# One transfer for the identity and the small tables, and a new order of the work around the first projection

## The reference, cut to what matters

```python
def _layernorm(x): return (x - mean(x)) / sqrt(var(x) + eps)

def attn(x, ln_w, ln_b, w_q, w_kv, w_o, theta):     # 16 heads of 16
    h = layernorm(x) * ln_w + ln_b
    q, k, v = h @ w_q, *split(h @ w_kv)
    q, k = rope(q, theta), rope(k, theta)            # angles: position * theta / 220 * fixed frequencies
    qk = einsum('bhkd,bhqd->bhkq', q, k) * 0.25
    t = 1 + qk + 0.5 * qk * qk                       # in place of exp
    attn = t / sum(t, -1)
    return einsum('bhkq,bhqd->bhkd', attn, v) @ w_o

def ffn(x, weight, bias):                            # both operands are rounded to a 6-bit grid,
    return dequant(x) @ dequant(weight).T + bias     # in blocks of 32 with a scale each

x = x + _layernorm(attn(_layernorm(x), ...))
x = x + _layernorm(ffn(_layernorm(x), weight, bias))
```

## Time and profile before

| | us |
|---|---|
| median of three runs | 634.89 |
| profiled execution | 634.73 |
| its span, first to last instruction | 632.9 |
| PE busy | 607.2 |
| DVE busy | 579.3 |
| ACT busy | 534.0 |
| POOL busy | 393.8 |

### The profile page before, as it was taken

The page is one execution under the profiler, slowest core; times in us unless marked ns, Lnnn a source line. Parts: engine busy times, 40 slices in busy tenths (PEclk is TensorE's granted clock), DMA queues, the critical chain, the costliest instruction groups (busy, mean ns, idle before and its releaser), DMA issues.

```text
span 632.9 us, 22530 instructions
## 1 busy us (share of the span) xinstructions
PE 607.2 (96%) x7588; PEld 470.3 (74%) x7588; DVE 579.3 (92%) x1425; ACT 534.0 (84%) x1505; POOL 393.8 (62%) x597
## 2 busy tenths in 40 slices
PE   8799999999999999999999999999999999999984
PEld 8677667777777787777777777777778777778763
DVE  5999999999999999999999999999999999987796
ACT  4357769898898989989899889899898888899983
POOL 2575366676666567766766777675765767653343
PEclk9999999999999999999999999999999999999996
DMA  7101131222232232223232231323233222230201
GB/s 251 35 3 39 24 76 23 66 77 74 60 95 63 76 91 64 76 49 93 73 105 62 79 83 42 108 55 97 62 83 84 68 49 52 69 85 20 68 27 51
DMA packets 55951, 43.64 MB, mean 69 GB/s; under 512 B 7200, under 2 KB 55712, under 8 KB 55840
## 3 DMA queue, kind: packets, MB, share of 16 engines
q1 hardware_dynamic: 55024, 41.42, 24.6%
q10 hardware_dynamic: 816, 0.79, 0.4%
HBM read 18.65 MB, written 8.39 MB: 43 GB/s over the span
## 4 chain that ended last, share of the span: by engine, by line
PE 87%; ACT 5%; issue 4%; DVE 3%; POOL 1%; POOLq 0%; ACTq 0%; DVEq 0%
PE ps_f L859 12%; PE ps_mt L1032 12%; PE ps_o L930 5%; PE ps_o L924 5%; PE ps_qk L783 5%; PE ps_qk L784 5%; PE ps_qk L786 5%; PE ps_w L783 4%; PE ps_tr L883 4%; PE ps_f L924 4%; PE ps_w L786 4%; PE ps_w L784 4%; PE ps_tr L783 3%; PE ps_tr L873 3%; PE ps_tr L786 2%
## 5 line engine op out<-in xcount | busy, mean ns | idle before, releaser
L1192 ACT ACTIVATE feat<-ps_f 128x512 f32<-128x512 f32 x256 | 147.5, 600 | 13.0 <-PE ps_f L859 12.4
L678 DVE TENSOR_TENSOR kf<-kf 128x672 f32<-128x672 f32 (+1 forms) x128 | 130.4, 1023 | 1.0
L859 PE MATMUL ps_f<-qT,selr 128*128 128x512 f32 x320 | 120.4, 426 | 2.0 <-ACT feat L1192 1.2
L1032 PE MATMUL ps_mt<-kf,vp 128*32 128x153 f32 x2048 | 79.6, 296 | 1.5 <-DVE kf L678 0.5
L1787 POOL TENSOR_TENSOR rs_f<-var_f,mhalf 128x1 f32<-128x1 f32 x64 | 47.9, 749 | 47.5 <-ACT squares_f L1326 46.5
L1787 POOL TENSOR_TENSOR rs_y<-var_y,mhalf 128x1 f32<-128x1 f32 x64 | 47.3, 740 | 41.9 <-ACT squares_y L1304 41.4
L1032 PEld LDWEIGHTS ps_mt<-kf,vp 128*32 128x32 f32 x2048 | 60.3, 109 | 16.7 <-issue 14.5
L1776 POOL TENSOR_TENSOR kf<-kf 128x128 f32<-128x128 f32 x64 | 36.6, 571 | 47.2 <-DVE kf L1543 47.2
L859 PEld LDWEIGHTS ps_f<-qT,selr 128*128 128x128 f32 x320 | 55.2, 188 | 13.3 <-ACT feat L1192 5.4
L1783 POOL TENSOR_TENSOR attT_l<-att,attT_h 128x256 fp32r<-128x256 f32 x56 | 45.0, 805 | 31.1 <-ACT attT_h L1233 31.0
L678 POOL TENSOR_TENSOR kf<-kf 128x224 f32<-128x224 f32 x64 | 58.2, 909 | 3.9 <-DVE kf L1548 3.8
(11 more groups left out here) (205 smaller groups left out, 1900.3 us busy)
## 6 DMA issues: line engine op xcount, KB each, us to landing
xc<-L_attn_x SPq DMA_DIRECT2D x16, 512.0 KB, 4.0
result<-fin SPq DMA_DIRECT2D x64, 128.0 KB, 1.9
xa<-L_attn_x SPq DMA_DIRECT2D x15, 512.0 KB, 4.0
heads_out<-osb SPq DMA_DIRECT2D x224, 32.0 KB, 2.0
shares<-sums SPq DMA_DIRECT2D x112, 64.0 KB
sums<-osb SPq DMA_DIRECT2D x224, 2.0 KB
wkqv<-L_attn_w_kv ACTq DMA_DIRECT2D x2, 256.0 KB, 4.6
xa<-L_attn_x SPq DMA_DIRECT2D x1, 384.0 KB, 6.1
```

The source lines that it names most:

```text
L678: return eng.tensor_tensor(dims(row, F_MAIN, [[FW, heads], [HD, NR - 1], [1, HD]]), dims(row, F_LIN, [[FW, heads], [0, NR - 1], [1, HD]]), ...
L859: pe.matmul(ps_f[i % 2][:, :], selr[:, i], queries, start=True, stop=True).then_inc(sel_done, 1)
L1032: mm = pe.matmul(ps_mt[qd // 2][VW * h:VW * (h + 1), (qd % 2) * NF:(qd % 2 + 1) * NF], vp[:, s2, qd * HQ + h], kf[:, s2, qd * HQ + h, 0:NF ...
L1192: act.activation(feat[:, p2, i], ps_f[i % 2][:, :], ACT.Square).then_inc(squared, 1)
```

## The change

Three things change. The identity and the small tables come in one transfer of 197 floats a partition with one semaphore, `cols_in`, and all who waited for `ident_in` wait for `cols_in`. The tile of ones is set by the first memset, with a semaphore `one_set` of its own, and PE begins on that; the others count to 15. The tables `ORDER` and `IDLE` are new for all five engines, over all 64 tiles. The diff without these tables:

```diff
+def sandwich(nc, x, w_q, w_kv, w_o, weight, bias, columns, selection, out):
...
             sp.dma_start(xa[:, 0, 0:1], x_seq[0][:, 0:1]).then_inc(x0_in, 16)
-            sp.dma_start(small[:, P:NSMALL], columns).then_inc(cols_in, 16)
-            sp.dma_start(ident, identity).then_inc(ident_in, 16)
+            sp.dma_start(small[:], columns).then_inc(cols_in, 16)
...
         def _(pe):
-            pe.wait_ge(setup_pool, 16)
+            pe.wait_ge(one_set, 1)
...
             def fold_kq():
 
+                pe.wait_ge(setup_pool, 15)
                 pe.wait_ge(wkq_in, 2 * 16)
...
             def turn_z(t):
                 if t.n == 1:
-                    pe.wait_ge(ident_in, 16)
                     pe.wait_ge(cols_in, 16)
...
-            act.wait_ge(setup_pool, 16)
+            act.wait_ge(setup_pool, 15)
             act.activation(warm[:], mhalf[:], ACT.Sin)
 
             def cast_identity():
-                act.wait_ge(ident_in, 16)
+                act.wait_ge(cols_in, 16)
...
             def turn_weights():
 
-                act.wait_ge(ident_in, 16)
+                act.wait_ge(cols_in, 16)
...
         def _(pool):
+            pool.memset(one[:], 1.0).then_inc(one_set, 1)
             pool.memset(mhalf[:], -0.5).then_inc(setup_pool, 1)
...
-            pool.memset(one[:], 1.0).then_inc(setup_pool, 1)
...
-            pool.wait_ge(setup_pool, 16)
+            pool.wait_ge(setup_pool, 15)
...
                 pool.tensor_scalar(lnwn[:], lnw, -((1.0 + EPS) ** -0.5), None, ALU.mult).then_inc(ln_scaled, 1)
-                pool.wait_ge(ident_in, 16)
...
-    arrays["identity"] = identity
     arrays["columns"] = np.ascontiguousarray(np.concatenate(
-        [columns, np.broadcast_to(theta, (P, 1)), ln_w.reshape(CH, P).T, ln_b.reshape(CH, P).T], axis=1), np.float32)
+        [identity, columns, np.broadcast_to(theta, (P, 1)), ln_w.reshape(CH, P).T, ln_b.reshape(CH, P).T], axis=1), np.float32)
...
-IDLE = {"fill": (1, 1, 1, 1, 1, 1, 4, 7, 10, 14, 15, 19, 23, 45,), "drain": ()}
+IDLE = {"fill": (2, 4, 6, 6, 6, 7, 7, 7, 8, 9, 16, 23, 40,), "drain": ()}
```

More of the change, by code:

```diff
@@ L98 @@
[L98 to L102 removed]
+        "attend": ((45, 59, 65, 79, 86, 104, 112, 130, 137, 149, 168, 187, 200, 214, 227, 244, 257, 272, 286, 300, 316,
+            330, 344, 359, 374, 388, 402, 416,), (26, 40, 54, 69,), (766, 780, 794, 808, 830, 835, 855, 866, 876, 891,
+            909, 919, 926,)),
@@ new lines @@
+        "high_kq": ((3,), (), ()),
+        "high_q": ((11, 18, 25, 33, 43, 55, 63, 69, 84, 94, 106, 117, 131, 149, 171, 187, 203, 216, 234, 253, 270, 291,
+            307, 323, 341, 362, 377, 394, 412, 432, 448, 465, 484,), (-86, -63, -49, -32,), (765, 784, 802, 818, 835,
+            853, 872, 889, 906, 926, 945, 961, 978, 998, 1014, 1039,)),
+        "high_v": ((6,), (), ()),
+        "sines": ((5,), (), ()),
+        "split_ffn_weight": ((127,), (), ()),
+        "split_wo": ((13,), (), ()),
[17 rows of a table added]
@@ L414, in dims @@
     return bass.AP(ap.tensor, ap.offset + offset, [list(ap.ap[0])] + [list(d) for d in free])
-def sandwich(nc, x, w_q, w_kv, w_o, weight, bias, identity, columns, selection, out):
+def sandwich(nc, x, w_q, w_kv, w_o, weight, bias, columns, selection, out):
     NS = x.shape[0]
```

404 lines of the change are left out of this document (197 added, 207 removed), and 88 rows, old and new, of the table ORDER.

## The result

The changed kernel took 635.88 us (median of 20 runs, 633.30 to 638.31), the kernel before, run beside it, 634.19 us (median of 20, 632.41 to 635.85). The ratio is 1.0022, its 95% interval 1.0013 to 1.0032. The forecast was 632.9 against 634.89, a ratio of 0.9969, so it is wrong in sign. The profiled execution took 636.04 us, its span 634.2 against 632.9.

The account below looks back on a forecast made before the run. The prediction took PE to bound the kernel from 100 to 550 us, with DVE the bound in the first 40. An earlier start would keep 2.0 us: 634.89 - 2.0 = 632.9 us, 8-in-10 range 630.7 to 635.9.

Parts of the forecast that it names:

- PE's first 14 us: Kernel start on PE: first product at about 1.0 us instead of 2.46, fold ending at 11.1 instead of 14.56.
- The merged transfer: Columns and identity in one load at the start: lands between 4.15 and 5.6 us, taken as 4.9.
- my lower bound: Start of PE's `fold_kq`: earliest 7.4 us, in a range of 7.4 to 7.9, taken as 7.6.
- DVE: DVE's first steps: angles end at 11.0 us, `low_kq` follows without `weight_scales` between, DVE ends about 1.4 us ahead.
- The wait of `normalise_x.1` for POOL: DVE, tile 1: idle for 1.0 us until POOL's tables are done, against 0.3 before.
- The lead: At the fourth `sum_features`: PE 2.4 us ahead, DVE 1.5; of this PE keeps 2.0 us.
- my own sign: Check on the start: if the fourth `sum_features` is not earlier than 41.54 us (forecast 40.4), the start's forecast is wrong.
- From there PE's work is the same in both: Behind the fourth `sum_features`: PE's work is unchanged, with one `fill` fewer, already counted.
- On SP nothing changes in the first 26 steps: SP queue at the start: its order is unchanged there, within edits costed at nothing.
- Rival (c): Slower: the new periodic order puts `low_h` one DVE step later, doubling PE's idle time; 636.9 us, chance 0.12.
- Rival (d), the clock: Slower: TensorE's full speed comes late, so the early fold runs at the slow pace; 636.2 us, chance 0.04.
- The sum: Whole kernel: 634.89 us less the 2.0 that PE keeps gives 632.9 us.

Follow-up runs that it names:

- e2: The changed kernel with all of SP's order put back to that of the kernel before, other engines as changed: 634.55 us, ratio 1.0003 to the kernel before.
- e5: The changed kernel with its new order only up to about tile 6; behind that, and on SP throughout, the order of before: 633.47 us, ratio 0.9969.
- e17: The changed kernel, unchanged, profiled and timed a second time: 637.08 us, ratio 1.0027 to the kernel before.

## Why the prediction was wrong, step by step

- **PE's first 14 us: right.** First product at 0.98 (forecast 1.0), `turn_z.0` at 6.11 (6.2), the fold from 7.12 (7.6, bounds 7.4 to 7.9, so 0.3 before the lower one) to 10.9 (11.1). The pace rose at 6.0, so the turn and the `fill` both ran at the later pace and were through at 6.94; my lower bound had the turn at the earlier one. The last 0.19 us were a wait for ACT's `wa`, written from 6.49 to 6.88, 0.1 later than in the kernel before. `project_kq.0` at 13.13 (13.4).
- **The merged transfer: right.** The first to use it starts at 4.68 (4.9, bounds 4.2 to 5.6), 3.5 us behind its issue at 1.18. Beside the 2.9 of the columns and the 3.9 of the identity the row length that the Trainium skill names (DMA: Bandwidth & Descriptors, Specifications: at least 512 B for line rate) doesn't show: the columns' rows are 276 B and landed soonest, the identity's are 512 B and landed latest, the merged ones are 788. Their sizes differ as well (34.5, 64 and 98.5 KB), so these rows neither show that rule nor refute it.
- **DVE: right within 0.6 us.** Angles from 5.63 to 11.46 (5.05 to 11.0), `low_kq.1` at 11.97 to 12.65 (11.8 to 12.45), `stats_x.1` 12.90 (12.75), `rope_cos.0` 15.81 (16.2). The 0.6 us are x of tile 0: it landed at 3.65 where it had landed at 3.07. The wait of `normalise_x.1` for POOL was 0.36, not 1.0: the tables were not as late.
- **The lead: right in size, but not made where I counted it.** Forecast: PE 2.4 us ahead, 2.0 kept. The first `sum_features` came 0.64 us earlier (0.5), `attend.3` 2.44. The fourth `sum_features` did not come earlier (41.66 against 41.54; forecast 40.4). By then PE had done three `select` and one `project_v` more, just as counted, which is 1.3 us of work, so it was 1.2 ahead there and not 2.4. By my own sign the count of the start was wrong at that row. The rest came behind it, where I had counted nothing: from 41.6 to 100 us PE idles 0.7 us less than before (1.1 against 1.8). That the sum agrees is in part luck, and where x of tile 0 lands at 3.02, close to the 3.07 of the rows that I counted from, the lead at tile 5 is 3.0 (e2).
- **"From there PE's work is the same in both": this is the step that failed.** The work is the same, its order is not, and I costed the order of 60 tiles at nothing. The forecast would have held for e5, the kernel to which that sentence applies: 0.9969, the lead kept to 0.2 us over 57 tiles. That the ratio is the very same is luck, since e5 starts from a larger lead and pays 1.4 us at its seam. In the changed kernel the order of the middle gives back 2.5 to 3.0 us in the same places in each trace and 0.1 to 2.4 more at one place. "On SP nothing changes in the first 26 steps" is true and beside the point: the later ones were priced at nothing too.
- **Rival (c) had the outcome and its test, not the mechanism.** It said slower by the new periodic order, with PE's idle time doubled: 3.95 became 7.85 us, 6.8 in the second trace. The price it worked out (636.9) is above the measured time; it left out the end, which in this trace is 1.5 us shorter from tile 60 on. But the wait it named, `low_h` one step late, is 0.3 us once, as before. The waits that grew are DVE's for POOL's `rs_y`, PE's for `fb` and those for which the profile names nobody ("issue"), and DVE's for the sums.
- **Rival (d), the clock: no part in it.** The fold's records ran at the later pace from the first (1.10, 1.05, 1.03 and 1.05 us for its four groups, against 1.03, 1.05, 1.03 and 1.05 in the kernel before). The row of the idle products shows the pace rise at 6.0 us here, 5.0 after they began; over the 17 traces of kernels with `one` set first it rose at 3.9 to 7.1. That the moment varies from run to run is what the Trainium skill states (TensorE: Matmul & The Clock Gate, Part 1), and here rows show it.
- **The sum.** -2.44 (lead at tile 3) + 5.28 (to tile 36) - 1.52 (from there to the end) = +1.32 us, the difference of the two spans.

What stays open: which pairs of steps in the new order make the 2.5 to 3.0 us that repeat. The waits say where they surface (POOL's `rs_y` before `add_attention`, DVE's `add_bias` before `project_out`), but the runs that moved these steps took the waits away without taking the loss away. Between 205 and 375 PE's idle time also explains only 3.6 of the 5.15 us; the rest is in records that PE counts as busy. It is not waiting, but mostly what stands behind what. From the start of each `select` to the start of PE's next record (93 of them, 207 to 373 us) 25.3 us pass in the kernel before and 30.8 in the changed one, of which 2.6 are idle; behind the turns of `z` it is 4.6 and 3.0. A `sum_features` follows a `select` 15 times where it did 8 times, at 0.40 us each, where a `select` behind a `select` takes 0.26 to 0.28. e17 has the same sums to 0.2 us.

## What to carry to other kernels

A list that orders the work of several engines is one object: its start can be exchanged at a price at the seam (1.4 us twice here, 5 once), its middle can't be judged by one engine or one step. When a change brings a new start and a new order behind it, price them apart, and run the new start with the old rest first; here that kernel was the gain (0.9969), and the rest was the loss. Compare when the bound engine begins the same step in both traces, tile by tile: busy shares differed by 0.1% here while the lead went from -3.1 to +2.8 us.
